# Two heads in one step of an fp32-split attention: the second head's scores built on top of the first's in PSUM

## What is computed

```
ctx = X @ We.T                                   # 32 channels, the same for every head
influence = jnp.einsum('bqe,bke->bqk', ctx, ctx)
Q, K, V = (heads(Wq), heads(Wk), heads(Wv))      # 16 heads of 16 channels
scores = jnp.einsum('bhqd,bhkd->bhqk', Q, K) * SCALE + 0.1 * influence[:, None]
attn = jax.nn.softmax(scores, axis=-1)
out = jnp.einsum('bhqk,bhkd->bhqd', attn, V)
out = out.transpose(0, 2, 1, 3).reshape(b, s, d) @ Wo.T
```

## Time and profile before

| | |
|---|---|
| median of 3 runs | 3754.39 us (3751.41 to 3756.76) |
| span of the profiled execution | 3752.2 us, 2.2 us under the median |
| PE busy | 3688.5 us, 98% |
| DVE, ACT, POOL busy | 3109.7, 2530.7 and 1104.0 us |
| mean granted PE clock | 0.998 of full speed |
| attention steps, first score product to last value product | from 416.1 to 3468.6 us of the span |

### The profile page before, as it was taken

The page is one execution under the profiler, slowest core; times in us unless marked ns, Lnnn a source line. Parts: engine busy times, 40 slices in busy tenths (PEclk is TensorE's granted clock), DMA queues, the critical chain, the costliest instruction groups (busy, mean ns, idle before and its releaser), DMA issues. The chain is left out here.

```text
span 3752.2 us, 74223 instructions
## 1 busy us (share of the span) xinstructions
PE 3688.5 (98%) x28483; PEld 2520.8 (67%) x28483; DVE 3109.7 (83%) x5242; ACT 2530.7 (67%) x4815; POOL 1104.0 (29%) x904
## 2 busy tenths in 40 slices
PE   5999999999999999999999999999999999999999
PEld 4998666666666666666666666666666666665898
DVE  7996888888888888888888888888888888884898
ACT  4764576677667766766676677667766776676565
POOL 5990122222222222221222222222222212222697
PEclk9999999999999999999999999999999999999999
DMA  3004310000010101010101000100000000012000
GB/s 133 19 20 177 95 34 14 19 13 20 13 21 13 21 13 21 13 21 13 21 13 21 12 20 13 20 14 18 16 18 15 18 16 19 16 24 63 37 20 22
DMA packets 245856, 105.79 MB, mean 28 GB/s; under 512 B 172800, under 2 KB 216224, under 8 KB 244512
## 3 DMA queue, kind: packets, MB, share of 16 engines
q1 hardware_dynamic: 240880, 97.34, 10.5%
q10 hardware_dynamic: 4656, 4.10, 0.4%
HBM read 63.80 MB, written 32.51 MB: 26 GB/s over the span
## 5 line engine op out<-in xcount | busy, mean ns | idle before, releaser
L1481 DVE TENSOR_REDUCE tops<-coarse 128x1 f32<-128x512 f32 x4048 | 2472.3, 684 | 483.1 <-PE coarse L1331 483.1
L1468 ACT ACTIVATE x_all<-fine 128x512 f32<-128x512 f32 x4096 | 2061.4, 625 | 786.0 <-PE fine L1352 786.0
L1352 PE MATMUL fine<-query_a,key_a 48*128 48x512 f32 x4096 | 1574.0, 427 | 0.3
L1352 PE MATMUL fine<-query_c,area 64*128 64x512 f32 x4096 | 1487.6, 393 | 0.0
L1352 PE MATMUL fine<-area,key_b 33*128 33x512 f32 x4096 | 1486.6, 392 | 0.0
L1331 PE MATMUL coarse<-key_a,query_a 48*128 48x512 f32 x4078 | 1422.1, 417 | 1.4 <-PEq L847 0.7
L1331 PEld LDWEIGHTS coarse<-key_a,query_a 48*128 48x128 f32 x4078 | 715.9, 185 | 489.7 <-issue 213.4
L1361 PE MATMUL o_ps<-x_all,vh 128*32 128x512 f32 x8192 | 984.7, 598 | 0.0
L1352 PEld LDWEIGHTS fine<-area,key_b 33*128 33x128 f32 x4096 | 763.6, 187 | 75.7
L1352 PEld LDWEIGHTS fine<-query_a,key_a 48*128 48x128 f32 x4096 | 752.0, 184 | 69.2 <-ACT x_all L1468 10.2
L1352 PEld LDWEIGHTS fine<-query_c,area 64*128 64x128 f32 x4096 | 756.9, 185 | 40.5
(11 more groups left out here) (227 smaller groups left out, 2951.5 us busy)
## 6 DMA issues: line engine op xcount, KB each, us to landing
area<-scratch_q SPq DMA_DIRECT2D x256, 64.0 KB, 2.0
area<-neg_max SPq DMA_DIRECT2D x1024, 0.5 KB, 2.0
query_a<-scratch_q SPq DMA_DIRECT2D x256, 32.0 KB, 1.8
key_b<-scratch_k SPq DMA_DIRECT2D x32, 256.0 KB, 3.4
x_all<-in_L_attn_X SPq DMA_DIRECT2D x4, 1024.0 KB, 12.6
spilled_x<-x_all SPq DMA_DIRECT2D x32, 128.0 KB, 1.7
scratch_q<-p_s_lo SPq DMA_DIRECT2D x16, 256.0 KB, 2.3
scratch_k<-p_s_lo SPq DMA_DIRECT2D x16, 256.0 KB, 2.9
```

Source lines behind the costliest of these rows:

```text
L1352: return pe.matmul(fine[i % 2][:, r, :], keys, query, start=at == 0, stop=at == CHUNKS - 1)
L1468: act.activation(probs[:, i % RING, r, :], fine[i % 2][:, r, :], ACT.Exp).then_inc(probs_ready, 1)
L1481: dve.tensor_reduce(tops[n][:, idx // KB, idx % KB:idx % KB + 1], bank, AX.X, ALU.max).then_inc(tops_ready, 1)
```

## The change

Heads are taken in pairs (`HEADS` = 2), so there are 64 steps, each of `NG` = 8 groups. A group has four score tiles of the first head (two pairs of key tiles, "slots" 0 and 1) and four of the second (slots 2 and 3, the same keys), so again 8 tiles, 8 coarse products and 8 value products, and again 512 groups in all.

- The first head's tiles are three products as before. The second head's are made in the same PSUM banks: after ACT has taken the first head's exponential, a product "old" with the negated query tile of the first head takes its head terms and maximum off, and a product "new" adds those of the second. Both have 49 rows (32 cross, 1 maximum, 16 high). So 8 tiles take 4 x 3 + 4 x 2 = 20 products, not 24.
- `WAVES` becomes `SEGMENTS`: 8 positions for the first head, then 6 for the second. 14 positions a group, not 16.
- `UNITS`, the coarse products of a step, is 64. The prologue makes `UNITS + AHEAD` = 80 of them, not 48. Those of the second head have 64 rows (`A_ROWS + DK`), with zeros in the first head's place. There are still three banks, with the same rule.
- Values are read in place from `v_all`, now 17 wide with the one stored in it; the copies to `vh` go. The four strips are two halves x two heads, so one level of adding is left (`add_halves` writes `total`), and `take_sums`, the sum's chain and `multiply` come once for two heads.
- POOL makes the negated query tile (`negate`), once a step.
- `Queries` holds each step's query tiles in slots of their own. SP loads them anew for every step: 18 DMAs at a step's start, then the first head's maxima, the sum's chain, a piece of the next pair's keys, the second head's maxima. DVE reduces for the maxima of each head, and inverts after unit 50 of 64.

The core of the diff (lines left out are marked "..."):

```diff
-WAVES = ["CCfffCfffCffffff", "ffffffCfffCfffCC"]
-PARTS = ["keys", "position", "low"]
-CHUNKS = len(PARTS)
+SEGMENTS = [("CffffffC", "fCfffffC"), ("CfCfff", "CffffC")]
+PARTS = [["keys", "cross", "low"], ["old", "new"]]
...
-NG = PAIRS // GROUP
-UNITS = QT * KB
+NG = PAIRS // 2
+UNITS = HEADS * QT * KB
...
 def add_halves(self, eng, s):
...
+        eng.tensor_copy(self.half[:, :], self.ot[2 * 32:2 * 32 + self.BOTH, :]).then_inc(self.moved, 1)
+        eng.wait_ge(self.moved, s + 1)
+        eng.tensor_tensor(self.total[:, :], self.ot[0:self.BOTH, :], self.half[:, :], ALU.add).then_inc(self.total_ready, 1)
...
+                def coarse_product(bank, t, head, q, r, kb):
+                    rows = half_rows(r, 0, A_ROWS + head * DK)
+                    return pe.matmul(bank, queries.coarse[head][t % queries.COARSE[head]][rows, q * P:(q + 1) * P],
+                                     key_a[t // NQB % 2][rows, kb * 512:(kb + 1) * 512], start=True, stop=True)
...
+                def wait_for_unit(t, idx):
...
+                    pe.wait_ge(tops_ready, UNITS * t + idx - COARSE + 1)
...
+                    else:
+                        rows = half_rows(r, 0, LOW_ROWS)
+                        keys, query = (key_low[0][kp][rows, cols], queries.negated[half][rows, :]) if what == "old" else (key_low[1][kp][rows, cols], queries.low[1][half][rows, :])
+                    return pe.matmul(fine[slot % 2][:, r, :], keys, query, start=what == "keys", stop=what in ("low", "new"), skip_group_check=what in PARTS[1])
...
+                    for r in range(2):
+                        for head in range(HEADS):
+                            kt, part = 2 * (2 * g + which) + r, HEADS * r + head
+                            last = pe.matmul(o_ps[32 * part:32 * part + DK + 1, :], v_all[:, head_of(s, head), kt, :], probs[:, ring(g, HEADS * head + which), r, :],
+                                             start=g == 0 and which == 0, stop=g == NG - 1 and which == 1)
...
+                                    if at == 0:
+                                        earlier = TILES_ENDED.index(((slot - 2) % SLOTS, r)) + 1 - (TILES_IN_GROUP if slot < 2 else 0)
+                                        pe.wait_ge(probs_ready, P_LEAD + TILES * s + TILES_IN_GROUP * g + earlier)
...
+                    pool.tensor_scalar(queries.negated[n][both, :], queries.low[0][n][both, :].bitcast(F32), -1.0, 1.0, ALU.mult, ALU.mult).then_inc(negated, 1)
```

More of the change, by code:

```diff
@@ L1032 @@
[L1032 to L1036, removed]
+    segments, ended, products, count = [], [], [0, 0], 0
+    for head, pattern in enumerate(SEGMENTS):
+        waves, chunks = [], [0, 0]
+        for k in range(max(len(half) for half in pattern)):
+            wave = []
+            for r in range(2):
+                if pattern[r][k] == "C":
+                    wave.append((r, None, "coarse", products[r], count))
+                    products[r] += 1
+                    count += 1
+                else:
+                    which, at = divmod(chunks[r], len(PARTS[head]))
+                    wave.append((r, HEADS * head + which, PARTS[head][at], at, None))
+                    chunks[r] += 1
+            wave.sort(key=lambda item: item[1] is None or item[3] == 0)
+            ended += [(slot, r) for r, slot, what, at, order in wave if slot is not None and at == len(PARTS[head]) - 1]
+            waves.append(wave)
+        segments.append(waves)
@@ L1037 @@
+    return segments, ended
+GROUP_SEGMENTS, TILES_ENDED = group_of_waves()
+UNITS_IN_GROUP = sum(half.count("C") for pattern in SEGMENTS for half in pattern)
+SLOTS = 2 * HEADS
+TILES_IN_GROUP = 2 * SLOTS
+INVERT_AFTER = 50
 A_ROWS = DE + DK
-KEY_PIECES = 4
 M_ROW = 2 * DK
+LOW_ROWS = M_ROW + 1 + DK
+KEY_PIECES = 5
 class Sums:
     ROWS = DK + 1
+    BOTH = 32 + DK + 1
     def __init__(self, nc, ctx, sem, inverses, at):
@@ L1067, in spread_inverse @@
     def spread_inverse(self, sp, s):
         sp.wait_ge(self.inv_saved, 16 * (s + 1))
[L1070 to L1075, removed]
+        for head in range(HEADS):
+            sp.dma_start(self.wide[32 * head:32 * head + DK, :],
+                         self.inverses[bass.ds(s, 1), head * QB:(head + 1) * QB].to_broadcast([DK, QB])).then_inc(self.spread, 16)
@@ L1077, in add_halves, with store @@
+    def store(self, sp, s, stored):
+        for head in range(HEADS):
+            first = head_of(s, head) * DK % P
+            sp.dma_start(self.at[first:first + DK, head_of(s, head) * DK // P, tokens(s)], self.wide[32 * head:32 * head + DK, :]).then_inc(stored, 16)
     def add_halves(self, eng, s):
-        upper = 32 + self.ROWS
         eng.wait_ge(self.ot_ready, s + 2)
-        eng.tensor_copy(self.half[:, :], self.ot[2 * 32:2 * 32 + upper, :]).then_inc(self.moved, 1)
+        eng.tensor_copy(self.half[:, :], self.ot[2 * 32:2 * 32 + self.BOTH, :]).then_inc(self.moved, 1)
@@ L1338, in wait_for_bank, with score_chunk @@
                     pe.wait_ge(tops_ready, UNITS * t + idx - COARSE + 1)
-                def score_chunk(s, half, kp, i, r, what, at):
-                    cols, queries = slice(i * P, (i + 1) * P), tokens(s)
+                def score_chunk(s, half, kp, slot, pair, r, what, at):
+                    cols = slice(pair * P, (pair + 1) * P)
                     if what == "low":
                         rows = half_rows(r, 0, M_ROW + 1)
-                        keys, query = key_b[kp][rows, cols], query_b[half][rows, :]
+                        keys, query = key_low[0][kp][rows, cols], queries.low[0][half][rows, :]
@@ L1367, in _ @@
                     pe.wait_ge(first.keys_loaded[j], first.KEY_DMAS)
-                for t in range(2):
-                    pe.wait_ge(first.queries_loaded[t], first.QUERY_DMAS)
+                for t, head in ((0, 0), (0, 1), (1, 0)):
+                    wait_for_coarse_queries(t, head)
                 done = 0
@@ L1506, in body @@
+                def body(s, half, kp):
                     for idx in range(AHEAD, UNITS):
                         reduce(s + 1, idx)
-                    if within(s + 1):
-                        max_rows(s + 1, 1 - half)
-                    for idx in range(0, INVERT_AFTER + 1):
+                        if idx == QT * KB:
+                            max_rows(s + 1, 0, QT * KB)
+                        if idx == INVERT_AFTER and s > 0:
+                            sums.invert(dve, s - 1)
+                    for idx in range(AHEAD):
```

572 lines of the change are left out of this document (285 added, 287 removed).

## The result

| | before | after |
|---|---|---|
| median | 3752.99 us (3751.41 to 3756.76, 4 runs) | 4068.55 us (4067.05 to 4069.55, 4 runs) |
| ratio, 95% interval | | 1.0843 (1.0827 to 1.0858): slower |
| span of the profiled execution | 3752.2 us | 4065.2 us |

What follows compares the result with a forecast made beforehand. PE's rate set the 5.95 us group, with DVE's and ACT's loops just under. 502 x 6.52 + 10 x 5.93 + 16 less 3053 is +295; +19 - 1 makes +313: 4065 us profiled, 4067 median, range 3980 to 4150.

Steps and rivals of the forecast that it cites:

- The group: Steps in attention: waiting for coarse banks stops PE 1.04 us, so a group takes 6.52 us, for 5.96 before.
- the 0.06 us to give a bank back: Coarse banks: PE's next weight load on a bank begins 0.06 us after DVE's reduction of that bank ends.
- the 0.10 for weights not loaded beneath other work: Coarse products on PE: one that had to wait lasts 0.50 us instead of 0.39, about 0.10 more.
- The second stop: Seventh coarse product of a group: waits for the fourth's reduction, ending at 3.46 us, and streams at 3.62.
- Value products: Value products at a group's end: 17 columns for 32 change nothing, 1.85 us stays, as each streams 512 columns.
- SP's list: SP's DMAs in a step: second head's maxima ready at 41 us, issued by 47, needed at 55; hidden, 6 to spare.
- The sum: Whole kernel: steps +295 us, prologue +19, output phase -1, together +313 us on the profiled execution's 3752, giving 4065.
- 10 x 5.93 + 16: Steps: ten last groups without coarse products take 5.93 us each, bound by exponentials; DVE's inversions add 64 x 0.25 = 16 us.
- Prologue ... 32 x 0.60 = 19: Prologue: 80 coarse products for 48, with DVE setting the pace at 0.60 us each, add 19 us.
- 0 to 2, taken as 0: Projection: POOL's extra fill and eight query loads instead of four cost 0 to 2 us, counted as 0.
- The rival on the clock: Groups in attention: PE's stops lower the granted clock; at 0.77 in every group, 770 us more in all; chance 0.03.
- Taking four positions out gave nothing: Last group before the change: 12 positions instead of 16, yet 4.08 us to its value products; reason to doubt a gain.

## Why the prediction was right

- **The group.** Forecast 6.52 us, measured 6.51, and each point on the way, with the measured one in brackets: third coarse product at 1.75 (1.75), weight load of the sixth at 2.92 (2.94), of the seventh 0.10 ahead of its 3.62, at 3.52 (3.53), values at 4.67 (4.67). It came from four rows of before: the reduction's length, its spacing, the 0.06 us to give a bank back, and the 0.10 for weights not loaded beneath other work. That both halves stop was right as well. The second stop ended as late as this 0.10 says: the seventh product's weight load and its record both start at 2012.86, so the load was not pulled ahead. The runs that shorten the reductions, move one product and bunch the old table bear the mechanism out, and not only the number.
- **Value products.** 1.84 for 1.85: 17 columns are as dear as 32; both stream 512.
- **SP's list.** The second head's maxima began to go out 41 us after the step's first DMA (2015.35 to 2056.36) and took about 6, in time for 55, as forecast; POOL's negation took 0.62 us and nobody waited for it.
- **The sum.** +313 forecast and +313 measured. That it is right to the microsecond is luck, since two errors of 12 us offset each other. The steps were put at +295 and gave +282.7; the start at +19 gave +30.7.
- **The step "10 x 5.93 + 16".** Groups without coarse products took 5.69 us, not 5.93, 2.4 us in all. That fits one product of 0.235 less behind the last exponential, two for three, but no run tests it. The inversion was sized at 0.25 us a step and cost 0.20 (a group with it took 6.69, its neighbours 6.49): 3 us. A group was 0.03 us shorter than worked out: 52.14 us for eight, inversion included, where the sum had 52.41. That is 14 us. Together these are 19 us less, of which some 7 came back in the first groups, which ran at half clock. From the first score product to the first value phase they took 15.5 us (446.8 to 462.3), where two groups up to their values are 9.3, and the next group 7.3.
- **The step "Prologue ... 32 x 0.60 = 19".** DVE did set the pace, but only while PE's clock held. At half clock a pair of products with its fillers takes 1.71 us for 1.20, and the prologue took 24.9 more, not 19. "0 to 2, taken as 0" for the projection was wrong too: the first product came 5.8 us later. POOL's fill cost 3.9 by holding up DVE, and the transposes behind that wait 0.9 more, at half clock. SP's loads cost 3.3. In the profiled execution 2.3 went off, since the stage ahead of the projection ended that much earlier, which differs by up to 3 us between kernels here whose code is the same up to there. The forecast had counted four more loads, but they are four more for each of two blocks. It was also silent on what the fill could do to DVE.
- **The rival on the clock** was right that the clock could fall and wrong about where. In the groups it stayed at 1.00 through stops of 1.2 us, and it fell in the prologue, where the page shows PE busy 5.00 of 5 us. The Trainium skill (TensorE: Matmul & The Clock Gate, on the HAM clock gate) ties the fast clock to activity, and the extra filler agrees with that (0.98 for 0.50 in 430:440).
- **"Taking four positions out gave nothing"** was the right warning. Had the forecast gone by PE's 98% and the 14 positions, it would have been 3525 us.

## What to carry to other kernels

Buffers that are handed back by another engine set a shortest distance between the n-th and the (n + buffers)-th use, here 1.17 us for three PSUM banks: count the work that lies between them in the issue order, and put a long phase that waits for neither engine there (here the value products) into the gap. Before crediting a cut on the busiest engine, look for a stretch where that work is already missing; if its period is no shorter, the cut buys nothing until the loops around it are loosened. And work moved to a start-up phase takes on that phase's conditions: its queue's free time, its clock, and what other engines do beside it.

## What was not expected of the hardware

The granted clock fell to 0.50 in a stretch in which the page calls PE busy 5.00 of 5 us, with a pair of half-array products and three fillers in each round of 1.2 us, and stayed at 1.00 in groups where PE stood still for 1 us at a time. A fourth filler in each round moved the fall some 10 us on. The busy share of the page did not tell what the clock would do.

A DVE operation on 128x32 elements took 4.13 or 5.07 us beside a fill by POOL, and 0.18 without it. In the changed kernel it ended at 303.15 us and POOL's fill at 303.11. A fill on an engine that has nothing else to do was not free here.
